# Window scores sorted by tile size, and the output projection behind the heads' transposes

## The chip, the cores and the metric

The kernel runs on one core of a Trainium2 chip. The metric is the device time of one execution in microseconds; lower is better. The engines are TensorE (PE for its matmuls, PEld for its weight loads, which overlap them), VectorE (DVE), ScalarE (ACT), GpSimd (POOL) and SyncE (SP), which issues the DMAs. Each engine works through its own instructions in order and waits on semaphores for the others.

## The reference

Thirty-two sequences of 128 tokens with 128 channels pass through one causal attention and one cross attention of 16 heads, and then through six layers of local attention and a gated MLP. The change lies in the local attention. Cut to what matters:

```python
for i in range(6):
    qkv = shift_tokens(x) @ Wqkv[i]                 # 128 -> 3 * 16 heads * 64
    q, k = rotary(l2norm(q) * q_scale), inverse_rotary(l2norm(k) * k_scale)
    # windows of 32 queries, each against its own 32 keys and the 32 before
    sim = einsum('bhwie,bhwje->bhwij', bq, bk2) * 8.0
    sim = where(mask, -max, sim)
    out = einsum('bhwij,bhwje->bhwie', softmax(sim, -1), bv2)
    x = out @ Wo[i] + x
    x = ffn_layer(shift_tokens(x)) + x
```

## The kernel before, in words

Each layer's local attention works through 128 groups: 32 sequences by four groups of four heads (64 channels each). One group enters in every step. A body of the loop holds `STEPS` = 8 steps, two sequences. The work of a group is spread over nine steps by hand-written lags (`WIN`), so one step of an engine holds pieces of several groups. TensorE's step, in the order of `win_products`:

- `win_project` (L735): queries and keys of group j, three matmuls of 512 columns, after it waits for the squares of the last group (`c_sq`).
- `win_turn_probs` (L791): two transposes of the probabilities of group j-7.
- `win_values` (L735): values of group j, three matmuls of 256 columns (`c_vproj`).
- `win_project_out` (L843): output projection of group j-8 from `prob_t`, four matmul records. It waits for ACT's copy of the head sums (`c_sum`) and, at a sequence's first group, for DVE's addition of the previous sequence's result into y (`c_yadd`).
- `win_heads` (L728): four transposes of the rotated queries and keys of group j-4. Ahead of the fourth, `sums_ready` makes PE wait for what the head sums below need: `c_vout` (ACT's copy of this step's values and turned probabilities), `c_scaled`, and for every second group `c_moved`.
- `win_mask` (L765): four bf16 matmuls with 64x64 tiles that put the band mask into PSUM.
- `win_scores` (L776): scores of group j-5, twelve matmuls in 24 records. A record is one pass of a matmul through the array; an f32 matmul of this kind has two. For each of two head pairs i, first two matmuls of 64x64 tiles (queries 0 to 63), then four of 64x32 tiles (queries 64 to 95, and 96 to 127). The last one signals `c_scores`.
- `win_sum_values` (L823): the head sums of group j-7, twelve matmuls with 64x64 tiles, 24 records.

A tile is the part of TensorE's array that one matmul uses, rows x columns. Matmuls with different tiles of one size run side by side.

ACT's step is `vout_all` (L1115, the copy of values and turned probabilities), `qk_t` (L1086, the copy of the turned heads), `squares` (L1095, after DVE's `by_sin`), four exponentials (L1104, after DVE's `top`) and `prob_t` (L1124, the copy of the head sums). DVE's step is `rsum` (L1595, after the exponentials), `prob` (L1605), `by_cos` (L1546), `by_sin` (L1554), `rotated` (L1563), `top` (L1587, the maxima, after `c_scores`), `norm` (L1570, after `squares`) and `norm2g` (L1580). In the fourth step of a sequence ACT also copies the next tokens (`xt_high`, L1075) behind `prob_t`, and DVE then makes `xt_low` (L1528) and adds to y (L1612) ahead of the next `rsum`. Of each layer's 128 steps, 123 run in `windowed`; the first five lie in the end of the layer before, beside its MLP. Eight more, without new projections, drain the pipeline (`drain`), and there the heads stand ahead of the output projection already.

Of the kernel before, what the change touches and what calls it, by code (L numbers as in the profile page):

```python
# [28 lines left out]
DH = 64  # L29
# [3 lines left out]
PAD = 32  # L33
# [39 lines left out]
KEYS = 2 * PAD  # L73
BASES = (0, PAD, 2 * PAD)
# [3 lines left out]
ENDED = GROUPS // STEPS  # L78
# [62 lines left out]
def has(index):  # L141

    return not isinstance(index, int) or index >= 0


def in_range(it, j, lag, n):

    return not isinstance(it, int) or 0 <= it * n[1] + j - lag < n[0]


def build(nc, x_in, ctx_in, a_w, a_m, b_wq, b_bq, b_wk, b_bk, b_wv, b_bv, b_wo, b_bo, wqkv, q_scale, k_scale,
          wo, ln_g, ln_b, w1, b1, w2, b2, const_d, out):
    with ExitStack() as stack:
        def sb(name, shape, dt=F32):
            return stack.enter_context(nc.sbuf_tensor(name, shape, dt))
# [11 lines left out]
        ident_b = sb("ident_b", [P, P], BF16)  # L167
        causal_b = sb("causal_b", [P, P], BF16)
        band_b = sb("band_b", [P, 2, KEYS], BF16)
# [88 lines left out]
        win_ps, sum_ps = [[t[:, :].rearrange("q (e n) -> q e n", e=2)[:, :, at:at + P] for t in (pair45, pair12)] for at in (0, P)]  # L258
# [16 lines left out]
        def sem(name):  # L275
            return stack.enter_context(nc.semaphore(name))
# [103 lines left out]
        c_scores = sem("c_scores")  # L380
# [70 lines left out]
        def here(it, j, lag):  # L451
            return in_range(it, j, lag, (GROUPS, STEPS))
# [125 lines left out]
        def _(pe):  # L578
# [138 lines left out]
            def win_heads(layer, it, j):  # L717
                if here(it, j, WIN.turn):
                    g = layer * GROUPS + it * STEPS + j - WIN.turn
                    jl = (j - WIN.turn) % STEPS  # L720
                    pe.wait_ge(c_unit, g + 1)
                    if has(it * STEPS + j - WIN.turn - 1):
                        pe.wait_ge(c_qk, g)
                    flat = rotated[jl % 4][:, :, :, :].rearrange("t a h d -> t (a h d)")
                    for k in range(4):
                        if k == 3 and not isinstance(it, int):
                            sums_ready(layer, it, j)
                        last = nc.tensor.transpose(heads_ps[:, k * P:(k + 1) * P], flat[:, k * P:(k + 1) * P], ident)  # L728
                    last.then_inc(c_heads, 1)

# [21 lines left out]
            def win_values(layer, it, j):  # L752
                if here(it, j, 0):
                    if has(it * STEPS + j - 1):

                        pe.wait_ge(c_vout, layer * VOUTS + it * STEPS + j)
                    gc = (j % NG) * HG * DH
                    split_product(value_ps[:, 2 * P:4 * P], j // NG, 2, slice(gc, gc + HG * DH)).then_inc(c_vproj, 1)

            def win_mask(layer, it, j):  # L760
                if here(it, j, WIN.scores):
                    for half in range(2):
                        for e in range(2):
                            rows, lower = slice(e * DH, (e + 1) * DH), half * DH
                            nc.tensor.matmul(win_ps[(j - WIN.scores) % 2][lower:lower + DH, e, :].rearrange("q (i k) -> q i k", i=2),  # L765
                                             ident_b[rows, rows], band_b[rows, half, :].unsqueeze(1).to_broadcast([DH, 2, KEYS]),
                                             start=True, stop=False, skip_group_check=True, tile_position=(e * DH, lower))

            def win_scores(layer, it, j):
                if here(it, j, WIN.scores):  # L770
                    jl = (j - WIN.scores) % STEPS
                    for i in range(2):
                        for lower, n, base in ((0, DH, BASES[0]), (DH, PAD, BASES[1]), (DH + PAD, PAD, BASES[2])):
                            for e in range(2):
                                rows, q0, k0 = slice(e * DH, (e + 1) * DH), i * P + lower, (2 + i) * P + base
                                last = nc.tensor.matmul(win_ps[jl % 2][lower:lower + n, e, i * KEYS:(i + 1) * KEYS],  # L776
                                                        qk_t[jl % 4][rows, q0:q0 + n], qk_t[jl % 4][rows, k0:k0 + KEYS],
                                                        start=False, stop=False, skip_group_check=True, tile_position=(e * DH, lower))
                    last.then_inc(c_scores, 1)

            def win_turn_probs(layer, it, j):
                if here(it, j, WIN.probs):
# [19 lines left out]
            def sums_ready(layer, it, j):  # L802

                if here(it, j, WIN.value):
                    jl = (j - WIN.value) % STEPS
                    if jl % 2 == 0:

                        pe.wait_ge(c_moved[jl // 2], 64 * (layer * ENDED + it + (1 if j >= WIN.value else 0)))
                    if here(it, j, WIN.scale):

                        pe.wait_ge(c_scaled, layer * GROUPS + it * STEPS + j - WIN.scale + 1)
                    pe.wait_ge(c_vout, layer * VOUTS + it * STEPS + j + 1)
# [15 lines left out]
            def win_project_out(layer, it, j):  # L828
                if isinstance(it, int) and it == 0 and j == STEPS - 1:
                    pe.wait_ge(s_wo_in, 16 * (layer + 1))  # L830
                if here(it, j, WIN.out):
                    m = layer * GROUPS + it * STEPS + j - WIN.out
                    jl = (j - WIN.out) % STEPS
                    b = it * 2 + (j - WIN.out) // NG
                    if jl % NG == 0:

                        if has(b - 1):
                            pe.wait_ge(c_yadd, layer * NB + b)
                        pe.wait_ge(c_xsplit, layer * NB + xt_before(b))
                    pe.wait_ge(c_sum, m + 1)  # L840
                    for i in range(2):
                        k = 2 * (jl % NG) + i
                        last = nc.tensor.matmul(acc_ps[:, 0:P], prob_t[(j - 1) % 2][:, i, :], wo_sb[:, k * P:(k + 1) * P],  # L843
                                                start=(k == 0), stop=(k == 2 * NG - 1))
                    if jl % NG == NG - 1:
                        last.then_inc(c_wo, 1)

            def xt_before(b):

                return min(NB, b + 4) if isinstance(b, int) else b + 4  # L850

            def win_products(layer, it, j):
                win_project(layer, it, j)
                win_turn_probs(layer, it, j)
                win_values(layer, it, j)
                win_project_out(layer, it, j)
                win_heads(layer, it, j)
                win_mask(layer, it, j)
                win_scores(layer, it, j)
                win_sum_values(layer, it, j)  # L860

            def win_step(layer, it, j):
                win_products(layer, it, j)
                win_turn_next(layer, it, j)
# [70 lines left out]
            def drain(layer):  # L935
                for j in range(WIN_DRAIN):
                    win_turn_probs(layer, ENDED, j)
                    win_heads(layer, ENDED, j)
                    win_project_out(layer, ENDED, j)
                    win_mask(layer, ENDED, j)  # L940
                    win_scores(layer, ENDED, j)
                    if j == 3:
                        mlp_turn(layer, 0, 1)
                    if j == 4:
                        mlp_turn(layer, 1, 0)
                    if j == 6:
                        mlp_up(layer, 1, 0)
                    win_sum_values(layer, ENDED, j)
                    if j == 6:
                        mlp_turn(layer, 1, 1)  # L950
                        mlp_up(layer, 1, 1)
                mlp_down(layer, 1, 1)
# [435 lines left out]
        def _(dve):  # L1388
# [193 lines left out]
            def win_max(layer, it, j):  # L1582
                if here(it, j, WIN.top):
                    m = layer * GROUPS + it * STEPS + j - WIN.top
                    slot = (j - WIN.top) % 2
                    dve.wait_ge(c_scores, m + 1)
                    nc.vector.tensor_reduce(top[slot][:, :].rearrange("q (e i) -> q e i", e=2), win_ps[slot].rearrange("q e (i k) -> q e i k", i=2),  # L1587
                                            AX_X, ALU.max, negate=True).then_inc(c_top, 1)

# [202 lines left out]
            with dve.Fori(0, NQ // 2) as q2:  # L1792
                for j in range(2):
                    q = q2 * 2 + j
# [9 lines left out]
                for j in range(2):  # L1804
                    q = q2 * 2 + j
# [45 lines left out]
```

## Time and profile before

| | |
|---|---|
| median of 3 runs | 4686.99 us (4685.81 to 4687.43) |
| profiled execution, its own time | 4686.16 us |
| its span | 4684.4 us |
| PE busy | 4212.9 us, 90% |
| PEld busy | 3257.4 us, 70% |
| DVE busy | 3681.5 us, 79% |
| ACT busy | 3240.9 us, 69% |
| POOL busy | 3109.8 us, 66% |

The span runs from the first instruction to the last; what lies around it is 1.8 us. Busy shares add up overlapping pieces, and matmuls are pipelined, so that the page's 90% for PE doesn't say that PE sets the pace. For that, the chain of waits is read in one step of the loop: which engine starts each piece as soon as something else has ended.

### The profile page before, as it was taken

What the parts mean: (1) busy time and instruction counts of PE and PEld (TensorE: products, weight loads), DVE (VectorE), ACT (ScalarE), POOL (GpSimd) and SP (SyncE); (2) the same over time, 40 slices, a digit from 0 to 9 for tenths busy, and PEclk for the clock granted to TensorE, in tenths of its full rate; (3) what the DMA queues carried; (4) which work ended last, traced back from release to release, by engine and by line L of the source; (5) the groups of instructions that cost most, each with busy time, mean ns of one, the idle gap of its engine ahead of it and who ended that gap; (6) DMA issues with size and microseconds to landing.
All of it is one profiled execution on the core that took longest, in us unless ns stands there. A gap on an engine that the chain in (4) does not pass through costs nothing.

```text
span 4684.4 us, 162974 instructions
## 1 busy us (share of the span) xinstructions
PE 4212.9 (90%) x60256; PEld 3257.4 (70%) x60256; DVE 3681.5 (79%) x9664; ACT 3240.9 (69%) x11601; POOL 3109.8 (66%) x2461
## 2 busy tenths in 40 slices
PE   7988868999889999899999899998899998999998
PEld 5666646777677777677777677776777776777776
DVE  7988877777777777687777687777777776877776
ACT  6889966777657777657777567776577775677774
POOL 4544457777657777667777577776677776677773
PEclk9999989999999999999999999999999999999999
DMA  2000001111111111111111111111111111111111
GB/s 75 0 0 1 0 14 33 29 29 28 33 48 30 29 29 29 32 49 29 28 28 29 35 47 29 29 29 32 49 30 29 28 29 33 35 29 29 29 30 41
DMA packets 301674, 140.09 MB, mean 30 GB/s; under 512 B 83988, under 2 KB 293778, under 8 KB 301458
## 3 DMA queue, kind: packets, MB, share of 16 engines
q1 hardware_dynamic: 301458, 137.25, 12.0%
q8 instruction: 130, 2.13, 0.2%
q14 instruction: 86, 0.70, 0.1%
HBM read 21.85 MB, written 2.10 MB: 5 GB/s over the span
## 4 chain that ended last, share of the span: by engine, by line
PE 40%; ACT 28%; DVE 22%; issue 8%; DVEq 1%; POOL 1%; SPq 0%; DMA 0%; ACTq 0%; POOLq 0%
ACT pair L1104 19%; PE pair L776 13%; PE bank L843 11%; DVE top L1587 7%; PE bank L728 6%; ACT prob_t L1124 6%; PE pair L899 3%; PE pair L765 3%; DVE top L1502 2%; DVE qk_parts L1477 2%; DVE by_cos L1546 1%; DVE by_sin L1554 1%; PE bank L915 1%; DVE by_sin L1470 1%; ACT prob L1029 1%
## 5 line engine op out<-in xcount | busy, mean ns | idle before, releaser
L1272 POOL TENSOR_TENSOR rnorm<-norm2g,neg_half 128x16 f32<-128x16 f32 x384 | 1115.4, 2905 | 366.7 <-DVE norm2g L1580 366.7
L1104 ACT ACTIVATE pair<-pair,top 128x64 f32<-128x64 f32 x3072 | 879.1, 286 | 390.1 <-DVE top L1587 390.1
L1264 POOL TENSOR_TENSOR rotated<-by_cos,by_sin 128x256 f32<-128x256 f32 x768 | 696.7, 907 | 567.4 <-DVE by_sin L1554 563.4
L1086 ACT ACTIVATE qk_t<-bank 128x512 f32<-128x512 f32 x768 | 459.2, 598 | 606.9 <-PE bank L728 606.6
L776 PE MATMUL pair<-qk_t 64*32 64x64 f32 (+1 forms) x18432 | 798.5, 230 | 0.0
L1285 POOL TENSOR_TENSOR rotated<-rotated,rnorm 128x512 f32<-128x512 f32 x768 | 784.6, 1042 | 0.5
L843 PE MATMUL bank<-wo_sb,prob_t 128*128 128x128 f32 x3072 | 548.8, 302 | 240.7 <-ACT prob_t L1124 131.2
L843 PEld LDWEIGHTS bank<-wo_sb,prob_t 128*128 128x128 f32 x3072 | 403.8, 191 | 398.2 <-ACT prob_t L1124 304.7
L735 PE MATMUL bank<-wqkv_high,xt_high 128*128 128x512 f32 (+1 forms) x1536 | 663.1, 432 | 17.2 <-ACT squares L1095 16.1
L776 PEld LDWEIGHTS pair<-qk_t 64*32 64x32 f32 (+1 forms) x18432 | 538.6, 114 | 175.5 <-issue 1.4
L1104 ACT ACTIVATION_READ_ACCUMULATOR pair<-pair,top 128x1 f32 x3072 | 625.7, 204 | 0.0
L1546 DVE TENSOR_TENSOR by_cos<-bank,rot_cos 128x512 f32<-128x512 f32 x768 | 522.7, 681 | 6.2 <-PE bank L735 6.1
L735 PE MATMUL bank<-wqkv_low,xt_high 128*128 128x512 f32 (+1 forms) x1536 | 524.7, 342 | 0.0
L1570 DVE TENSOR_REDUCE norm<-squares 128x8 f32<-128x512 f32 x768 | 520.2, 677 | 3.5 <-ACT squares L1095 3.5
L1554 DVE TENSOR_TENSOR by_sin<-bank,sin_now 128x512 f32<-128x512 f32 x768 | 522.8, 681 | 0.0
L735 PE MATMUL bank<-wqkv_high,xt_low 128*128 128x512 f32 (+1 forms) x1536 | 521.7, 340 | 0.0
L1115 ACT ACTIVATE vout_all<-bank 128x512 f32<-128x512 f32 (+1 forms) x810 | 468.0, 578 | 76.1 <-PE bank L735 58.3
L1095 ACT ACTIVATE squares<-bank 128x512 f32<-128x512 f32 x768 | 456.0, 594 | 42.6 <-DVE by_sin L1554 39.5
L1254 POOL TENSOR_TENSOR kz_parts<-qk_parts,cst 128x512 fp32r<-128x512 f32 x256 | 266.2, 1040 | 308.4 <-DVE qk_parts L1477 308.4
L728 PE MATMUL bank<-cst,rotated 128*128 128x128 f32 x3072 | 469.0, 276 | 0.0
L1587 DVE TENSOR_REDUCE top<-pair 128x4 f32<-128x256 f32 x768 | 325.7, 424 | 177.8 <-PE pair L776 159.7
L823 PE MATMUL pair<-vout_all 64*64 64x64 f32 x6096 | 423.0, 232 | 33.7 <-issue 33.7
(152 smaller groups left out, 9044.2 us busy)
## 6 DMA issues: line engine op xcount, KB each, us to landing
vmoved<-vout_all SPq DMA_DIRECT2D x1152, 64.0 KB, 2.1
ctx_all<-vout_all SPq DMA_DIRECT2D x384, 64.0 KB, 2.1
wqkv_sb<-in_L_ffn_Wqkv_dram SPq DMA_DIRECT2D x36, 256.0 KB, 3.8
ctx_all<-y SPq DMA_DIRECT2D x48, 128.0 KB
ctx_all<-y SPq DMA_DIRECT2D x48, 127.0 KB
wo_sb<-in_L_ffn_Wo_dram SPq DMA_DIRECT2D x6, 512.0 KB, 10.2
out_dram<-y SPq DMA_DIRECT2D x8, 256.0 KB, 3.5
w_sb<-in_L_ffn_W_dram SPq DMA_DIRECT2D x6, 341.0 KB, 3.2
```

What stands on the lines that cost most here:

```text
L728: last = nc.tensor.transpose(heads_ps[:, k * P:(k + 1) * P], flat[:, k * P:(k + 1) * P], ident)
L735: last = nc.tensor.matmul(dst, a[slot][:, :], w[:, which, cols], start=(n == 0), stop=(n == 2))
L776: last = nc.tensor.matmul(win_ps[jl % 2][lower:lower + n, e, i * KEYS:(i + 1) * KEYS], qk_t[jl % 4][rows, q0:q0 + n], qk_t[jl % 4][rows, k ...
L843: last = nc.tensor.matmul(acc_ps[:, 0:P], prob_t[(j - 1) % 2][:, i, :], wo_sb[:, k * P:(k + 1) * P], start=(k == 0), stop=(k == 2 * NG - 1))
L1104: last = nc.scalar.activation(at, at, ACT.Exp, bias=top[jl % 2][:, h:h + 1], accum_out=psum_raw[jl % 2][:, h:h + 1])
L1264: nc.gpsimd.tensor_tensor(rotated[j % 4][:, 1, :, :], by_cos[j % 2][:, 1, :, :], by_sin[j % 2][:, 1, :, :], ALU.add).then_inc(c_rot, 1)
L1272: nc.gpsimd.tensor_tensor(rnorm[slot][:, :, :].rearrange("t g n -> t (g n)"), norm2g[slot][:, :, :].rearrange("t g n -> t (g n)"), neg_hal ...
L1285: nc.gpsimd.tensor_tensor(at, at, rnorm[slot][:, i, :].unsqueeze(2).to_broadcast([P, 2 * HG, DH]), ALU.mult).then_inc(c_unit, 1)
L1546: nc.vector.tensor_tensor(by_cos[j % 2][:, :, :, :], got, table(rot_cos, layer).unsqueeze(2).to_broadcast([P, 2, HG, DH]), ALU.mult).then_ ...
L1554: nc.vector.tensor_tensor(rows(by_sin[j % 2]), got, rows(sin_now), ALU.mult).then_inc(c_sin, 1)
L1570: nc.vector.tensor_reduce(pair[:, :, 0:1], squares[:, :, :], AX_X, ALU.add).then_inc(c_nrm2, 1)
L1587: nc.vector.tensor_reduce(top[slot][:, :].rearrange("q (e i) -> q e i", e=2), win_ps[slot].rearrange("q e (i k) -> q e i k", i=2), AX_X, A ...
```

## The change

The masks and scores of a group are now sorted by tile size. `win_upper_scores` does queries 64 to 127 with 64x32 tiles: four masks, then eight matmuls. `win_lower_scores` does queries 0 to 63 with 64x64 tiles: two masks, then four matmuls. The head sums, 64x64 too, follow. The masks are six matmuls instead of four, since the upper half's two are cut into four. Each of the two calls signals `c_scores`, and DVE waits for both. In a step of `windowed`, the heads' transposes come ahead of the output projection, and the waits of `sums_ready` move from the heads' fourth transpose to between the two matmuls of the output projection. In the drain only the sorting applies.

```diff
@@ win_heads
                     for k in range(4):
-                        if k == 3 and not isinstance(it, int):
-                            sums_ready(layer, it, j)
@@ scores
-            def win_scores(layer, it, j):
+            def win_scores(layer, it, j, tiles):
                 if here(it, j, WIN.scores):
                     jl = (j - WIN.scores) % STEPS
+                    for lower, n, base in tiles:
+                        for e in range(2):
+                            rows, upper = slice(e * DH, (e + 1) * DH), lower // DH
+                            at = e * DH + lower % DH
+                            nc.tensor.matmul(win_ps[jl % 2][lower:lower + n, e, :].rearrange("q (i k) -> q i k", i=2),
+                                             ident_b[rows, at:at + n], band_b[rows, upper, :].unsqueeze(1).to_broadcast([DH, 2, KEYS]),
+                                             start=True, stop=False, skip_group_check=True, tile_position=(e * DH, lower))
                     for i in range(2):
-                        for lower, n, base in ((0, DH, BASES[0]), (DH, PAD, BASES[1]), (DH + PAD, PAD, BASES[2])):
+                        for lower, n, base in tiles:
...
+            def win_upper_scores(layer, it, j):
+                win_scores(layer, it, j, ((DH, PAD, BASES[1]), (DH + PAD, PAD, BASES[2])))
+
+            def win_lower_scores(layer, it, j):
+                win_scores(layer, it, j, ((0, DH, BASES[0]),))
@@ win_project_out
                     for i in range(2):
                         k = 2 * (jl % NG) + i
+                        if i and not isinstance(it, int):
+                            sums_ready(layer, it, j)
@@ win_products
+                win_heads(layer, it, j)
                 win_project_out(layer, it, j)
-                win_heads(layer, it, j)
-                win_mask(layer, it, j)
-                win_scores(layer, it, j)
+                win_upper_scores(layer, it, j)
+                win_lower_scores(layer, it, j)
                 win_sum_values(layer, it, j)
@@ VectorE, win_max
-                    dve.wait_ge(c_scores, m + 1)
+                    dve.wait_ge(c_scores, 2 * m + 2)
```

TensorE's queue in a step of the loop, before, from the output projection to the scores. In these rows `bank` and `pair` are PSUM, the sizes are contraction or output rows by columns, and the semaphores waited for stand in brackets:

```order
L843 MATMUL bank<-wo_sb,prob_t 128x128 [waits c_sum_copied]
L843 MATMUL bank<-wo_sb,prob_t 128x128
L728 MATMUL bank<-cst,rotated 128x128 [waits c_qk_ready,c_unit]
L728 MATMUL bank<-cst,rotated 128x128 x2
L812 REGISTER_ALU [waits c_scaled,c_values_moved3]
L728 MATMUL bank<-cst,rotated 128x128 [waits c_vout_ready]
L765 MATMUL pair<-band_b,ident_b 64x128 x4
L776 MATMUL pair<-qk_t 64x64 x2
L776 MATMUL pair<-qk_t 32x64 x4
L776 MATMUL pair<-qk_t 64x64 x2
L776 MATMUL pair<-qk_t 32x64 x4
```

And the same place now:

```order
L726 MATMUL bank<-cst,rotated 128x128 [waits c_qk_ready,c_unit]
L726 MATMUL bank<-cst,rotated 128x128 x3
L847 MATMUL bank<-wo_sb,prob_t 128x128 [waits c_sum_copied]
L814 REGISTER_ALU [waits c_scaled,c_values_moved3]
L847 MATMUL bank<-wo_sb,prob_t 128x128 [waits c_vout_ready]
L765 MATMUL pair<-band_b,ident_b 32x128 x4
L772 MATMUL pair<-qk_t 32x64 x8
L765 MATMUL pair<-band_b,ident_b 64x128 x2
L772 MATMUL pair<-qk_t 64x64 x4
```

The transposes have moved ahead of the wait for `c_sum`, the wait for `c_vout` has moved from the last transpose into the output projection, and the tile size changes once inside the scores instead of three times.

In the drain, TensorE's queue of a step before, from the heads to the first head sums:

```order
L728 MATMUL bank<-cst,rotated 128x128 [waits c_qk_ready,c_unit]
L728 MATMUL bank<-cst,rotated 128x128 x3
L843 MATMUL bank<-wo_sb,prob_t 128x128 [waits c_sum_copied]
L843 MATMUL bank<-wo_sb,prob_t 128x128
L765 MATMUL pair<-band_b,ident_b 64x128 x4
L776 MATMUL pair<-qk_t 64x64 x2
L776 MATMUL pair<-qk_t 32x64 x4
L776 MATMUL pair<-qk_t 64x64 x2
L776 MATMUL pair<-qk_t 32x64 x4
```

There the order of heads and output projection stays, and only the mask and score rows are sorted, as above.

## Rows read from the trace of the kernel before

**Rows 1.** Chain of waits: start us, us, engine and line; one loop step.

```profile
2498.72 0.71 PE bank L843 x4
2499.43 0.44 PE bank L728 x4
...
2500.98 0.44 DVE top L1587
2501.44 1.15 ACT pair L1104 x7
2502.61 0.40 ACT prob_t L1124
```

**Rows 2.** Timeline of PE: start us, us, line, output<-inputs, tile, idle before and releaser.

```profile
2503.06 0.71 PE L843 MATMUL bank<-wo_sb,prob_t 128*128 128x128 f32 x4 [0.19 <-ACT prob_t L1124]
```

**Rows 3.** Timeline of DVE over one body of eight steps, maxima and rotated queries.

```profile
2486.98 0.42 DVE L1587 TENSOR_REDUCE top<-pair 128x4 f32<-128x256 f32 x1 [0.26 <-PE pair L776]
...
2492.31 0.42 DVE L1587 TENSOR_REDUCE top<-pair 128x4 f32<-128x256 f32 x1
...
2496.14 0.42 DVE L1563 TENSOR_TENSOR rotated<-by_cos,by_sin 128x256 f32<-128x256 f32 x1
2496.65 0.42 DVE L1587 TENSOR_REDUCE top<-pair 128x4 f32<-128x256 f32 x1
...
2502.76 0.18 DVE L1595 RECIPROCAL rsum<-psum_raw 128x4 f32<-128x4 f32 x1 [0.47 <-ACT pair L1104]
...
2504.63 0.43 DVE L1563 TENSOR_TENSOR rotated<-by_cos,by_sin 128x256 f32<-128x256 f32 x1
2505.32 0.42 DVE L1587 TENSOR_REDUCE top<-pair 128x4 f32<-128x256 f32 x1 [0.26 <-PE pair L776]
...
2509.83 0.42 DVE L1563 TENSOR_TENSOR rotated<-by_cos,by_sin 128x256 f32<-128x256 f32 x1
2510.37 0.42 DVE L1587 TENSOR_REDUCE top<-pair 128x4 f32<-128x256 f32 x1
...
2523.38 0.42 DVE L1587 TENSOR_REDUCE top<-pair 128x4 f32<-128x256 f32 x1 [0.26 <-PE pair L776]
```

**Rows 4.** Timeline of DVE at the first layer's start, ahead of the first output projection.

```profile
722.44 0.42 DVE L1587 TENSOR_REDUCE top<-pair 128x4 f32<-128x256 f32 x1
...
726.09 0.42 DVE L1563 TENSOR_TENSOR rotated<-by_cos,by_sin 128x256 f32<-128x256 f32 x1
726.43 0.42 DVE L1587 TENSOR_REDUCE top<-pair 128x4 f32<-128x256 f32 x1
```

**Rows 5.** The same stretch on PE and on ACT.

```profile
722.75 0.50 PE L735 MATMUL bank<-wqkv_high,xt_high 128*128 128x512 f32 x1 [1.63 <-ACT squares L1095]
...
724.39 0.60 ACT L1115 ACTIVATE vout_all<-bank 128x512 f32<-128x512 f32 x1 [0.20 <-PE bank L735]
```

**Rows 6.** Timeline of PE in narrow windows: masks, scores and head sums by tile.

```profile
2504.14 0.25 PE L765 MATMUL pair<-band_b,ident_b 64*64 64x128 bf16 x4
2504.22 0.28 PE L776 MATMUL pair<-qk_t 64*64 64x64 f32 x4
...
2504.43 0.32 PE L776 MATMUL pair<-qk_t 64*32 64x64 f32 x8
...
2504.67 0.33 PE L776 MATMUL pair<-qk_t 64*64 64x64 f32 x4
...
2505.18 0.27 PE L823 MATMUL pair<-vout_all 64*64 64x64 f32 x1
...
2505.51 0.22 PE L823 MATMUL pair<-vout_all 64*64 64x32 f32 x1
```

**Rows 7.** Timeline of ACT, the copy of the values in that step.

```profile
2502.91 0.60 ACT L1115 ACTIVATE vout_all<-bank 128x512 f32<-128x512 f32 x1
```

**Rows 8.** Waits in all, longest first: us in total, times, longest us.

```profile
PEld bank L843 <- ACT prob_t L1124: 304.7, 641, 1.2
...
DVE top L1587 <- PE pair L776: 159.7, 493, 2.6
```

More of the change, by code:

```diff
@@ L758, in win_values @@
                     split_product(value_ps[:, 2 * P:4 * P], j // NG, 2, slice(gc, gc + HG * DH)).then_inc(c_vproj, 1)
[L760 to L767, printed above, removed]
-            def win_scores(layer, it, j):
+            def win_scores(layer, it, j, tiles):
                 if here(it, j, WIN.scores):
                     jl = (j - WIN.scores) % STEPS
+                    for lower, n, base in tiles:
[5 more added lines that the diff above has]
+                                             start=True, stop=False, skip_group_check=True, tile_position=(e * DH, lower))
                     for i in range(2):
-                        for lower, n, base in ((0, DH, BASES[0]), (DH, PAD, BASES[1]), (DH + PAD, PAD, BASES[2])):
+                        for lower, n, base in tiles:
                             for e in range(2):
@@ L939, in drain @@
                     win_project_out(layer, ENDED, j)
-                    win_mask(layer, ENDED, j)
-                    win_scores(layer, ENDED, j)
+                    win_upper_scores(layer, ENDED, j)
+                    win_lower_scores(layer, ENDED, j)
                     if j == 3:
```

## The prediction, on record before the changed kernel ran

> **What bounds the kernel now.** I first read the chain of waits in one step of the loop [rows 1]. It goes round in a circle: output projection 0.71 us, heads' transposes 0.44, masks and scores from 2499.87 to 2500.98, the maxima on DVE 0.44, the exponentials on ACT 1.15, the copy `prob_t` 0.40. Then the next output projection starts at 2503.06 [rows 2], 4.34 us after the last one. So PE's 90% busy is not the bound: PE stands still for 0.19 us ahead of the output projection, released by ACT's `prob_t` [rows 2], and the wait shows in nearly every step as the hold of the weight load, 641 times [rows 8]. The transposes stand in the circle only because they are queued behind the output projection.
>
> Second, DVE over one body of eight steps [rows 3]. From the maxima at 2486.98 to those at 2523.38 it takes 36.40 us. In most steps DVE is idle 0.26 us until PE's scores are done; the view of waits has that 493 times, 159.7 us [rows 8]. The body's steps, from maxima to maxima, are 5.33 us (a sequence's end, where y is added, and the loop's branch), 4.34, 4.33, 4.34, 5.05 (the other sequence's end) and three of about 4.34. The 5.33 step already ends with the maxima right behind other DVE work, without idle time. It gains nothing.
>
> **What would be next.** DVE and ACT have a circle of their own: maxima, exponentials, `rsum`, `prob`, `by_cos`, `by_sin`, `rotated`, maxima. The trace shows it unhindered at a layer's start, before any output projection is there: maxima at 722.44, `rotated` at 726.09, maxima 0.34 behind it at 726.43 [rows 4]. That is 3.99 us. In the steady loop the same pieces read: maxima 2500.98 [rows 1] to `rotated` 2504.63 is 3.65, plus 0.34 is again 3.99, where the maxima actually start at 2505.32, 4.34 after [rows 3]. No order on PE can go below that. In one step the circle is longer: from 2492.31 to `rotated` 2496.14 plus 0.34 is 4.17 instead of 4.34 [rows 3]. At the sequence's end in mid-body it is from 2505.32 to 2509.83 plus 0.34, that is 4.85 instead of 5.05 [rows 3].
>
> **The change part by part.** *Heads ahead of the output projection.* The transposes leave the circle through `prob_t`: 4.34 less 0.44 is 3.90 for it. While PE transposes, `prob_t` is being copied, so the 0.19 of standing still is covered too. `c_unit`, which the transposes wait for, comes from GpSimd in the group's third or fourth step, and they read it in the fifth; the buffer they write was emptied one step before. I cost that at nothing.
>
> *The moved wait.* `sums_ready` now stands ahead of the second half of the output projection. Behind it on PE are the masks, the scores and the head sums, and DVE's maxima wait for the scores. The last to come is `c_vout`. Before, the copy `vout_all` ran from 2502.91 to 2503.51 [rows 7], 0.75 after `rsum` started at 2502.76 [rows 3], and the wait stood late enough to be free. Now it decides. The state to come is shown at the layer's start, where the values' projection is held by `squares` (1.63 idle) and the copy starts at 724.39 [rows 5], 1.95 after the maxima of 722.44 [rows 4]. So, counted from the maxima: copy 1.95 to 2.55, PE released at about 2.60. From there to the masks: before, four records of output projection and four transposes took from 2503.06 [rows 2] to 2504.14 [rows 6], 1.08; less six records of 0.11 (0.44 by four [rows 1]) that leaves 0.42 with the tile switch. Masks at 3.02.
>
> *Sorting.* In the old order the sets start at 2504.22 (64x64), 2504.43 (64x32), 2504.67 (64x64), and the head sums at 2505.18 after one more 64x32 set; masks at 2504.14 [rows 6]. From 2504.43 to 2504.67 is 0.24 for two passes and a change of size. The head sums, all of one size, put six passes of four records between 2505.18 and 2505.51 [rows 6], about 0.06 a pass. So a change of size costs about 0.12 more than going on. New: masks 0.08, four upper passes with one change 0.24 + 2 x 0.06 = 0.36, lower masks 0.08 (taken like the first ones), four lower passes 0.24: 0.76 us to the head sums instead of 1.04. The last score pass starts 0.70 after the masks. Before it started 0.89 after them (2505.18 less the 0.15 of the last change and start). That is 0.19 sooner. The maxima started 1.18 after the masks (2505.32 less 2504.14); now they could 0.99 after. The two masks more are in this. Bounds for the section, as seen by the maxima: 0.19 gained if the passes keep the 0.06, nothing gained if the changes removed had only hidden something else; I take 0.19, since the 0.06 is measured on tiles used again and again, as here.
>
> Sum for a plain step: 3.02 + 0.99 = 4.01 by way of the moved wait, 3.99 by way of DVE, 3.90 - 0.19 = 3.71 by way of `prob_t`. The step is 4.01, and PE's own work, 4.34 - 0.19 - 0.28 = 3.87, fits in.
>
> Here a figure of the Trainium skill speaks against the change. The head sums' 24 records between 2505.18 and 2505.51 are 14 ns apart on average [rows 6]. The Trainium skill (TensorE: Matmul & The Clock Gate, "Wait — 56ns, not 53.3ns?") gives about 62 ns of sequencer time for each matmul when hardware decode is off; the trace disagrees. By that price the two masks more would put 0.12 into the path, the step would be 4.13, and the time would come to some 4550. By these rows I give that price a chance of 0.01, inside the case between forecast and first rival.
>
> **The sum.** Per body: 5.33 stays; 4.34 to 4.17 saves 0.17; five plain steps save 0.33 each, 1.65; the sequence's end 5.05 to 4.85 saves 0.20, since PE is held there by y and has its scores ready before DVE wants them. Together 2.02 us of 36.40. There are 123 steps per layer in `windowed`, 6 layers, 738 steps, 92 bodies: 186 us. The first steps of a layer already run at 3.99 and the code ahead of the loop has the same steps, so this may be a few us too much. In the drain only the sorting acts, 0.19 in three or so steps whose chain goes through the scores, times 6: 3 us. The two attentions ahead and the MLP are untouched. 4686.16 - 186 - 3 = 4497. The profiled execution is 0.8 below the median of the runs, which I neglect.
>
> **The rivals.**
>
> *The wait keeps the bound, the sorting gives nothing.* The plain step is then 4.01 + 0.19 = 4.20. Six steps save 0.14 each, the sequence's end 0.20: 1.04 by 92 is 96 us, 4590. For it: the path through `vout_all` and the one through DVE differ by 0.02 us only, so every hundredth that the path is underestimated shows. Against: the 0.06 per pass.
>
> *Slower.* The passes on the same tiles don't follow at 0.06. Upper passes now run four in a row on the same four tiles, and lower ones four in a row on only two, with weights changed each time. Six such intervals stand ahead of the last pass. The step is back at 4.34 when they cost 0.33 more, that is at 0.115 each instead of 0.06. At 0.16 the step is 4.01 + 6 x 0.10 = 4.61, 0.27 longer in six steps of eight, and the time is about 4686 + 149 = 4835. The head sums at 0.06, with the same four tiles reused, speak against it; for two tiles of 64 columns the trace has only pairs of passes.
>
> *No change.* Another chain holds 4.34, and heads and sorting are both hidden by it. It would need a wait that is now within 0.01 of the circle without being in it. The 3.99 at a layer's start speaks against it, though there the output projection is missing. 4678 to 4695.
>
> *More than forecast.* The steps in which DVE's circle takes 4.17 or longer may do so only because of how PE's work falls. If they too went to 3.99, and the 5.33 by as much, another 0.36 x 92 = 33 us: 4464.
>
> That the change does not do what it says is ruled out by the order of PE's instructions, which shows both moves in the loop's body.
>
> **Chances.** Forecast, 4475 to 4530: 0.64. Wait or passes between, 4530 to 4600: 0.21. More than forecast: 0.05. No change: 0.04. Slower: 0.06. The range for 8 in 10 reaches from 4464, the further case of DVE, to 4590, where sorting gives nothing. Under 0.2%, 9 us, a measurement of this kernel can't tell from no change; faster by more than that has 0.90, within it 0.04, slower 0.06.
>
> **What would show it.** The maxima should follow `rotated` by 0.34 in plain steps, with no idle time left to PE in most of them, and stand 3.99 to 4.03 apart. The idle time in front of the output projection's first record should be gone, and a new one should stand inside it, ended by ACT's `vout_all`. ACT's wait for the heads should nearly vanish and its wait for `by_sin` ahead of `squares` grow; PE's projection should start to wait for `squares`. From the first mask to the first head sum it should be 0.76 us. If that stretch is 0.9 or more, the sorting step is wrong; if it is right and the maxima still wait for PE, the moved wait is.

## The result

| | before | changed |
|---|---|---|
| median | 4686.62 us (4 runs, 4685.81 to 4687.43) | 4498.4 us (4 runs, 4497.05 to 4500.48) |
| ratio | | 0.9599, 95% interval 0.9582 to 0.9615 |
| span of the profiled execution | 4684.4 us | 4498.7 us |
| granted clock, mean | 0.984 | 0.980 |

The change makes the kernel 188 us faster. The forecast was 4497, in a range of 4464 to 4590. The clock doesn't explain the gain: the granted clock is a little lower now, 0.980 instead of 0.984. With its two levels, 2.4 and 1.2 GHz, that is 180 instead of 150 us at the lower one, so by this estimate it costs at most some 15 us.

The timeline of DVE in the changed kernel shows one plain step, from maxima to maxima. It answers to [rows 3] and [rows 4]:

```profile
2403.98 0.42 DVE L1591 TENSOR_REDUCE top<-pair 128x4 f32<-128x256 f32 x1
...
2405.76 0.18 DVE L1599 RECIPROCAL rsum<-psum_raw 128x4 f32<-128x4 f32 x1 [0.22 <-ACT pair L1108]
...
2407.63 0.42 DVE L1567 TENSOR_TENSOR rotated<-by_cos,by_sin 128x256 f32<-128x256 f32 x1
2407.97 0.42 DVE L1591 TENSOR_REDUCE top<-pair 128x4 f32<-128x256 f32 x1
```

The maxima start 0.34 us behind `rotated` and 3.99 after the last ones, and no idle time stands in front of them. That is DVE's own circle. PE in the same step, in the timeline (the last two rows overlap):

```profile
2406.06 0.98 PE L847 MATMUL bank<-wo_sb,prob_t 128*128 128x128 f32 x4
2406.96 0.24 PE L765 MATMUL pair<-band_b,ident_b 64*32 64x128 bf16 x4
2407.03 0.39 PE L772 MATMUL pair<-qk_t 64*32 64x64 f32 x16
2407.35 0.24 PE L765 MATMUL pair<-band_b,ident_b 64*64 64x128 bf16 x2
2407.43 0.34 PE L772 MATMUL pair<-qk_t 64*64 64x64 f32 x6
2407.56 0.27 PE L825 MATMUL pair<-vout_all 64*64 64x64 f32 x1
...
2407.61 0.22 PE L772 MATMUL pair<-qk_t 64*64 64x64 f32 x2
```

The last pass of the scores starts 0.65 us after the masks and ends at 2407.83. In a run further down DVE does wait for the scores in nearly every step (maxima first), and there it starts 0.92 after the first mask. So the maxima could have started at 2407.88; they did at 2407.97. PE is ahead of DVE, but by 0.09 us only.

The waits in all (us, times, longest): those that the forecast named, ACT's for the values' projection, and the one that was to go:

```profile
ACT squares L1099 <- DVE by_sin L1558: 640.6, 757, 1.9
...
PEld bank L733 <- ACT squares L1099: 146.9, 447, 2.0
PEld bank L847 <- ACT vout_all L1119: 123.0, 464, 0.4
...
ACT vout_all L1119 <- PE bank L733: 61.5, 41, 2.9
...
DVE top L1591 <- PE pair L772: 31.2, 27, 2.3
```

The view counts 27 waits of DVE for the scores instead of 493 [rows 8]. ACT's wait for `by_sin` was 39.5 us before. PE waits now for `squares`, ahead of the projection, and for `vout_all`, inside the output projection.

ACT's wait for the turned heads, 606.6 us before, has all but gone. The page's group of that copy, to its right the idle time before it:

```profile
L1090 ACT ACTIVATE qk_t<-bank 128x512 f32<-128x512 f32 x768 | 469.8, 612 | 5.4 <-PE bank L726 5.1
```

### The profile page after: what moved, and what is told of

It reads as the page before. It is cut to its first block, busy times and chain, and to the rows that moved or that the text cites. A ratio compares the mean times of both kernels' runs of the same rounds, so it can differ in the third digit from the quotient of the medians.

```text
span 4498.7 us, 166670 instructions
## 1 busy us (share of the span) xinstructions
PE 4006.1 (89%) x61792; PEld 3187.6 (71%) x61792; DVE 3629.1 (81%) x9664; ACT 3219.3 (72%) x11601; POOL 3113.0 (69%) x2461
## 4 chain that ended last, share of the span: by engine, by line
PE 44%; DVE 28%; ACT 16%; issue 10%; DVEq 1%; POOL 1%; SPq 0%; ACTq 0%; DMA 0%; POOLq 0%
PE bank L733 16%; DVE by_cos L1550 7%; DVE by_sin L1558 6%; PE bank L847 6%; PE bank L726 6%; ACT pair L1108 6%; ACT squares L1099 5%; PE pair L903 4%; PE pair L772 3%; PE bank L793 3%; PE pair L765 3%; DVE top L1506 3%; DVE top L1591 2%; DVE qk_parts L1481 2%; PE pair L825 2%
## 5 line engine op out<-in xcount | busy, mean ns | idle before, releaser
L847 PE MATMUL bank<-wo_sb,prob_t 128*128 128x128 f32 x3072 | 691.6, 315 | 163.8 <-DVE y L1616 56.1
L847 PEld LDWEIGHTS bank<-wo_sb,prob_t 128*128 128x128 f32 x3072 | 451.2, 190 | 355.3 <-ACT vout_all L1119 123.0
L772 PE MATMUL pair<-qk_t 64*32 64x64 f32 (+1 forms) x18432 | 610.6, 218 | 0.0
L825 PE MATMUL pair<-vout_all 64*64 64x64 f32 x6096 | 453.3, 226 | 37.8 <-issue 37.8
L1090 ACT ACTIVATE qk_t<-bank 128x512 f32<-128x512 f32 x768 | 469.8, 612 | 5.4 <-PE bank L726 5.1
L772 PEld LDWEIGHTS pair<-qk_t 64*32 64x32 f32 (+1 forms) x18432 | 459.9, 116 | 0.0
L733 PEld LDWEIGHTS bank<-wqkv_high,xt_high 128*128 128x128 f32 x1536 | 290.5, 189 | 207.6 <-ACT squares L1099 146.9
```

The source lines that it names most:

```text
L733: last = nc.tensor.matmul(dst, a[slot][:, :], w[:, which, cols], start=(n == 0), stop=(n == 2))
L825: last = nc.tensor.matmul(out_ps[e * DH:(e + 1) * DH, lower:lower + width], values_of(j, i, e, n), vout[j][rows, e * P + lower:e * P + low ...
```

## The experiments

Each run is set beside the kernel before, timed next to it on the same chip. A step is the median time from maxima to maxima of the plain steps of a body; where two values stand, they alternate. Gains over the kernel before are taken against the time in the same row. The chips differ by up to 6 us for the same kernel, so between rows of different chips the ratios are the safer measure.

| kernel | median us | before, beside it | ratio, 95% interval | plain step us |
|---|---|---|---|---|
| changed | 4498.4 | 4686.6 | 0.9599 (0.9582 to 0.9615) | 3.99 |
| sorting only | 4534.5 | 4689.4 | 0.9670 (0.9654 to 0.9686) | 4.07 |
| move only | 4612.5 | 4689.4 | 0.9834 (0.9818 to 0.9850) | 4.18 and 4.26 |
| wait left in the heads | 4666.5 | 4689.4 | 0.9950 (0.9933 to 0.9967) | 4.19 and 4.28 |
| changed, maxima first | 4439.3 | 4689.4 | 0.9462 (0.9446 to 0.9478) | 3.90 and 3.99 |
| the same, third wait apart | 4436.1 | 4683.6 | 0.9473 (0.9457 to 0.9488) | 3.90 and 3.98 |
| before, maxima first | 4700.5 | 4683.6 | 1.0036 (1.0022 to 1.0050) | 4.34 |
| changed, by_cos first | 4618.1 | 4683.6 | 0.9858 (0.9841 to 0.9874) | 4.07 and 4.17 |
| changed, both edits | 4875.9 | 4683.6 | 1.0411 (1.0394 to 1.0429) | 4.50 and 4.67 |
| sorting only, two changes | 4614.4 | 4684.4 | 0.9851 (0.9834 to 0.9867) | 4.23 |
| sorting only, lower first | 4545.9 | 4684.4 | 0.9706 (0.9690 to 0.9723) | 4.10 |

### Sorting alone, moving alone

Sorting only, against the changed kernel:

```diff
                     for k in range(4):
+                        if k == 3 and not isinstance(it, int):
+                            sums_ready(layer, it, j)
...
-                        if i and not isinstance(it, int):
-                            sums_ready(layer, it, j)
...
-                win_heads(layer, it, j)
                 win_project_out(layer, it, j)
+                win_heads(layer, it, j)
```

> The changed kernel with the order of before for heads and output projection and with the wait for the values' copy in the heads' fourth transpose; only the sorting by tile size stays. If PE's circle through prob_t (4.34 us a step) sets the pace here, the sorting shortens it by what the scores finish sooner: 0.19 as forecast, 0.24 if the last score pass starts 0.65 us after the masks as the changed kernel's trace shows. Steps of 4.15 or 4.10, five or six of eight, and the time 4560 to 4570 or 4535 to 4545. If the gain came from the move alone and the sorting only followed, the step stays at 4.34 and the time at 4687.

4534.5 us: 155 us of gain, most of what both edits bring. The chain of waits shows PE's circle again, as in [rows 1], with the scores shortened:

```profile
2250.22 0.71 PE bank L847 x4
2250.93 0.44 PE bank L728 x4
2251.37 0.17 PE pair L767 x4
2251.53 0.22 PE pair L774 x16
2251.76 0.17 PE pair L767 x2
2251.93 0.18 PE pair L774 x6
2252.21 0.44 DVE top L1591
2252.67 1.12 ACT pair L1108 x7
2253.85 0.40 ACT prob_t L1128
2254.29 0.71 PE bank L847 x4
```

From output projection to output projection it is 4.07, and 0.27 of the 4.34 has gone. The masks and scores take 0.84 (2251.37 to 2252.21) where they took 1.11. The expectation's second figure, 4.10, was near; its first, from the forecast's 0.19, was too small.

Move only, against the kernel before:

```diff
-                        if k == 3 and not isinstance(it, int):
-                            sums_ready(layer, it, j)
...
+                        if i and not isinstance(it, int):
+                            sums_ready(layer, it, j)
...
+                win_heads(layer, it, j)
                 win_project_out(layer, it, j)
-                win_heads(layer, it, j)
```

> The kernel of before with heads ahead of the output projection and the wait moved into it; masks and scores unsorted. The path through the moved wait was put at 4.01 with the sorting; without it 4.20, and the time 4590. The changed kernel's trace has the scores ready 0.07 us before DVE takes them (a path of 3.92), and unsorted scores end 0.24 later: 4.16, and the time 4570 to 4580. If DVE's own circle of 3.99 were all that counts once the heads are out of the way, the time would be 4500 as with the sorting.

4612.5 us, 77 us of gain. The plain steps take 4.18 and 4.26 in turn; the forecast's 4.20 for this very case is met in the step. In time it came out 22 us slower than 4590, since the sequences' ends (5.01 and 5.39 against 4.86 and 5.33 in the changed kernel) and the step behind the longer one (4.34 against 4.17) are longer too. A step without idle time in front of the maxima would be 3.99, so here PE's path is the bound, and the expectation's third case, 4500, falls.

Together the two make 155 + 77 = 232 us, but both at once gained 188. The missing 44 us are put down to DVE's circle, which is tested below. Only some 11 of them are missing in the bodies: there sorting alone saves 1.69 us, moving alone 0.51 and both 2.08, by the medians of the eight steps. Much of the rest is missing in a layer's first and last steps, which take 3.99 by the move alone already and 3.99 in the changed kernel too.

### Where the wait stands

The wait left in the heads, against the changed kernel:

```diff
                     for k in range(4):
+                        if k == 3 and not isinstance(it, int):
+                            sums_ready(layer, it, j)
...
-                        if i and not isinstance(it, int):
-                            sums_ready(layer, it, j)
```

> The changed kernel with the wait for the values' copy left in the heads' fourth transpose, as before, heads ahead of the output projection. If that wait is as close to the bound as the trace says (path 3.92 by it), one transpose and four records instead of two then stand behind it, 0.44 us more: a step of 4.36, and the time 4670 to 4700, the whole gain gone. If the wait is not near the bound, the time stays at 4498.

4666.5 us: only 23 us of the gain are left, by a wait that stands three matmul records earlier in PE's queue. The waits in all show the new first line on PE, and beside it a second one that was not expected, for DVE's `prob`:

```profile
PEld bank L728 <- ACT vout_all L1119: 494.5, 563, 1.5
...
PE bank L728 <- DVE prob L1609: 210.1, 198, 1.6
```

A transpose and the whole output projection now stand behind the wait. The plain step is 4.19 and 4.28, less than the 4.36 expected. The expectation had an error: three records of 0.11 us more behind the wait are 0.33, not 0.44, and 3.92 + 0.33 = 4.25 is what was measured. The sequences' ends, 5.17 and 5.66 against 4.86 and 5.33, add to it. A whole body takes 36.4 us, as in the kernel before; the 23 us come from a layer's first and last steps, which run at 3.99. So inside the loop the place of this wait is worth as much as the whole change.

### The floor under DVE's circle

DVE's step, against the changed kernel:

```diff
-                win_rotate_queries(layer, it, j)
                 win_max(layer, it, j)
+                win_rotate_queries(layer, it, j)
                 win_norms(layer, it, j)
```

> The changed kernel with DVE's maxima ahead of the rotated queries, which takes 0.34 us out of DVE's circle (3.99 to 3.65) and leaves all work in. If DVE's circle sets the changed kernel's pace, the next bound is PE's path through the values' copy at 3.92: 0.07 less in six steps of eight, up to 0.17 more in the first two steps of a body, 40 to 70 us in all, 4430 to 4460. If PE's path is the bound already (4.01 as forecast), the time stays within 10 us of 4498.

4439.3 us, 59 less than the changed kernel, by an edit that only swaps two instructions on DVE. DVE's timeline now has the maxima waiting for PE:

```profile
2209.42 0.42 DVE L1591 TENSOR_REDUCE top<-pair 128x4 f32<-128x256 f32 x1 [0.37 <-PE pair L772]
...
2213.37 0.42 DVE L1591 TENSOR_REDUCE top<-pair 128x4 f32<-128x256 f32 x1 [0.26 <-PE pair L772]
...
2217.36 0.42 DVE L1591 TENSOR_REDUCE top<-pair 128x4 f32<-128x256 f32 x1 [0.38 <-PE pair L772]
```

So DVE's circle did set the changed kernel's pace, and the path through the moved wait lies at 3.90 and 3.99 in turn (here 3.95 and 3.99), not at 4.01. With the floor lowered, the sum also closes roughly: 250 us of gain against 232 for the two edits apart, of which some 27 come from steps that DVE bound before as well (5.33 to 5.13 and 4.17 to 4.08, times 92 bodies). This version beats both kernels.

The same swap in the kernel before:

> The kernel of before with the same edit on DVE, maxima ahead of the rotated queries. In the kernel before, PE's circle through prob_t is the bound (4.34) and DVE's circle of 3.99 has 0.35 to spare; only the first step of a body and the one at its end are bound by DVE. So 0.17 at the most in one or two steps of eight, 0 to 30 us: 4660 to 4690. If DVE's order mattered in itself, as it did for the changed kernel (59 us), the gain would be the same 59 us, 4630.

4700.5 us, 17 slower. Where DVE's circle is not the bound, the swap brings nothing, as expected; the 5.33 step, which DVE does bound, falls to 5.23. That the swap costs something on the whole was not expected. One step of eight takes 4.62 instead of 4.34, and the rotated queries now stand behind a wait of DVE for PE:

```profile
2318.20 0.42 DVE L1587 TENSOR_REDUCE top<-pair 128x4 f32<-128x256 f32 x1 [0.63 <-PE pair L776]
2318.54 0.41 DVE L1563 TENSOR_TENSOR rotated<-by_cos,by_sin 128x256 f32<-128x256 f32 x1
```

By which way the later queries reach that one step was not followed up.

The alternation of 3.90 and 3.99 might come from the third wait of every second group. That wait apart, against the changed kernel with the maxima first:

```diff
-                    if jl % 2 == 0:
+                    if jl % 2 == 0 and isinstance(it, int):
...
+                        if k == 2 and not isinstance(it, int) and here(it, j, WIN.value) and (j - WIN.value) % 2 == 0:
+                            pe.wait_ge(c_moved[(j - WIN.value) % STEPS // 2], 64 * (layer * ENDED + it + (1 if j >= WIN.value else 0)))
...
```

> The changed kernel with the maxima first, and with the wait for the moved values (every second group) taken out of the output projection and put ahead of the heads' third transpose; the waits for prob and for the values' copy stay. With the maxima first, the plain steps take 3.90 and 3.99 in turn. If the third wait behind the output projection's first half costs the 0.09, all plain steps come to 3.90 and the time falls by 4 x 0.09 x 92, 33 us at the most, 4405 to 4425. If the alternation is DVE's, nothing changes, 4439.

4436.1 us, and 3.90 and 3.98 in turn. The ratios, 0.9473 and 0.9462, lie in each other's intervals: no difference. That wait is not the cause. The timeline of the run with the maxima first shows that the 0.09 arises ahead of it: the copy `vout_all` starts 2.00 us after the maxima in the steps of 3.99 (2213.37 to 2215.36) and 1.90 after them in those of 3.90 (2226.10 to 2228.00). What delays the copy in every second step stays open.

### DVE's idle time filled, and what that shows

DVE's step, against the changed kernel:

```diff
+                win_cos(layer, it, j)
                 win_recip(layer, it, j)
                 win_scale(layer, it, j)
-                win_cos(layer, it, j)
                 win_sin(layer, it, j)
```

> The changed kernel with DVE's by_cos ahead of rsum and prob, where DVE stands idle for the exponentials (0.47 a step). That takes as much as 0.47 out of DVE's circle by another edit. If the floor under DVE's circle is PE's path through the values' copy (3.90 and 3.99 in turn, as with the maxima first), the time comes to the same 4430 to 4450. If the maxima's early start did something else in that run, the two differ: 4498 still, or well under 4430.

4618.1 us, 120 slower than the changed kernel. The expectation was wrong. The moved wait is not for the values' copy alone. `sums_ready` waits for `prob` of this step as well, and with `by_cos` (0.68 us) in front of it, where the changed kernel has 0.41 us of idle time on average (233.4 us in 564 waits), `prob` ends later. The plain steps take 4.07 and 4.17 instead of 3.99, and the sequences' ends 5.34 and 5.83 instead of 4.86 and 5.33: the ends make up 0.99 of some 1.6 us that a body gets longer. The timeline of PE at a sequence's end, the second half of the output projection:

```profile
2201.71 0.48 PE L847 MATMUL bank<-wo_sb,prob_t 128*128 128x128 f32 x2 [0.41 <-DVE y L1616]
2203.25 0.48 PE L847 MATMUL bank<-wo_sb,prob_t 128*128 128x128 f32 x2 [1.06 <-DVE prob L1609]
2203.66 0.28 PE L765 MATMUL pair<-band_b,ident_b 64*32 64x128 bf16 x4
2203.73 0.64 PE L772 MATMUL pair<-qk_t 64*32 64x64 f32 x16
```

In the whole run PE's records have 195.1 us of idle time ended by `prob` on this line, in 367 waits. The changed kernel has 30.8 us in 92 waits. On top of it TensorE's clock falls. The same sixteen records took 0.39 in the changed kernel and 0.64 here. The stretches around it, with the busy time of each engine and the granted clock after POOL's:

```profile
2200.00:2203.20 3.20, 1.78 (x13) 1.26 (x11) 1.79 (x6) 1.98 (x8) 2.90 (x1) 1.00 0.13 31
2203.20:2207.20 4.00, 3.95 (x61) 3.21 (x62) 2.13 (x5) 2.17 (x10) 2.98 (x3) 0.57 0.00 0
2207.20:2212.00 4.80, 4.47 (x79) 3.85 (x78) 4.00 (x10) 3.09 (x12) 1.54 (x2) 1.00 0.22 51
```

The clock is the smaller part. In the whole run it is 0.974 against 0.980, some 60 us more at the lower level, which by this estimate cost 30 of the 120 us at the most.

Both edits together:

> Both edits on DVE in the changed kernel. If PE's path is the floor, the second edit brings nothing: 4425 to 4445. If DVE's circle were still the bound with one edit, it falls by another 0.3 us a step, 4250 to 4350.

4875.9 us, slower than the kernel before, and far from both figures expected. With both edits DVE waits for PE's scores before it rotates the queries, and PE waits for DVE's `prob` before it makes the scores of the next step:

```profile
DVE top L1591 <- PE pair L772: 628.8, 715, 2.3
...
PE bank L847 <- DVE prob L1609: 488.6, 599, 1.5
```

So DVE's circle is not a sum of pieces from which any may be taken: what stands in the place of the piece decides who waits next.

### What a change of tile size costs

Against sorting only, the upper scores of the second head pair (`pairs`) moved behind the lower ones. The diff leaves out how `win_scores` uses its three new arguments:

```diff
...
             def win_upper_scores(layer, it, j):
-                win_scores(layer, it, j, ((DH, PAD, BASES[1]), (DH + PAD, PAD, BASES[2])))
+                win_scores(layer, it, j, ((DH, PAD, BASES[1]), (DH + PAD, PAD, BASES[2])), pairs=(0,))
...
-                win_scores(layer, it, j, ((0, DH, BASES[0]),))
+                win_scores(layer, it, j, ((0, DH, BASES[0]),), signal=False)
+                win_scores(layer, it, j, ((DH, PAD, BASES[1]), (DH + PAD, PAD, BASES[2])), masks=False, pairs=(1,))
```

> The sorting-only kernel (order and wait of before) with one change of tile size more inside the scores: upper masks and upper scores of the first pair, lower masks and all lower scores, upper scores of the second pair, then the head sums. Same matmuls. Steps took 4.34 with three changes inside the scores and 4.07 with one. If each change ahead of the last score pass costs the same, half the gain goes, a step of 4.20 and a time of 4605 to 4615. If the sorting's gain comes from something else (the masks, two tiles instead of six at a time), the time stays near 4534 or jumps back to 4687.

4614.4 us and a step of 4.23. Three changes of size inside the scores make 4.34, two 4.23, one 4.07, with the same scores and, between the last two, the same masks too. PE's timeline in this kernel:

```profile
2286.89 0.24 PE L767 MATMUL pair<-band_b,ident_b 64*32 64x128 bf16 x4
2286.96 0.28 PE L774 MATMUL pair<-qk_t 64*32 64x64 f32 x8
2287.17 0.24 PE L767 MATMUL pair<-band_b,ident_b 64*64 64x128 bf16 x2
2287.25 0.64 PE L774 MATMUL pair<-qk_t 64*64 64x64 f32 x16
```

One more change costs 0.16. Of that 0.14 is the later start of the last score pass, 0.79 instead of 0.65 after the masks; the rest lies between that pass and the maxima. From three changes to two only 0.11 is gained; there the kernel with three has two masks fewer, which may be the difference of 0.05, but no run takes the masks apart.

Lower tiles first, against sorting only:

```diff
+                win_lower_scores(layer, it, j)
                 win_upper_scores(layer, it, j)
-                win_lower_scores(layer, it, j)
...
```

The same swap is made in the drain.

> The sorting-only kernel with the lower 64x64 tiles first and the upper 64x32 tiles behind them, so that the size changes once inside the scores, as there, and once more between scores and head sums. If PE's circle ends at the scores, a change behind them is hidden in PE's slack, and the time is that of sorting only, 4525 to 4545. If PE's whole work counts, 0.15 to 0.3 a step come back, 4580 to 4640.

4545.9 us, a step of 4.10. A change of size now stands between scores and head sums as well, and it is hidden there. The ratio is 0.0036 above that of sorting only, 17 us, just clear of both intervals: 0.03 a step. The change behind the scores isn't the cause of these 0.03, for the last score pass starts 0.65 after the masks in both kernels. They lie between that pass and the maxima, which start 0.29 after it here, where it is one of 64x32 tiles, and 0.27 after it in the kernel with sorting only, where it is one of 64x64. So PE's work after the scores is off the path, and the work up to them is on it.

## Why the prediction was right, point by point

**The bound before.** The circle through the output projection, the transposes, the scores, the maxima, the exponentials and `prob_t` [rows 1] was the bound. Sorting alone shortens it by the 0.27 by which the scores finish sooner. Moving alone takes the transposes out of it, and the path through the moved wait takes over at 4.18 and 4.26.

**The next bound.** The circle of DVE and ACT at 3.99, read from a layer's start [rows 4] and from the pieces of a steady step [rows 3], is exactly what the changed kernel runs at. Body by body its steps are 3.99 five times, 4.17, 4.86 and 5.33, where the forecast had 4.01, 4.17, 4.85 and 5.33. The swap of two DVE instructions, which shortens that circle and leaves PE's queue as it is, confirms that it was the bound, by 59 us.

**The moved wait.** The forecast had the path through `vout_all` at 4.01 and took it for the bound by 0.02. That was wrong, if by little: the path is 3.90 and 3.99, and DVE's circle is the bound. Of the difference 0.05 is the copy, which starts 1.90 after the maxima (2403.98 to 2405.88) and not 1.95, and 0.07 is the sorting, below. The step from the released wait to the masks was 0.42 in the sum, and it is 0.41: in the changed kernel the second half starts at 2402.56 and the masks at 2402.97. That the wait is that near to the bound is shown by the run in which it stays in the heads, and by the one in which `prob` comes later. What the forecast didn't see is how near the second of its semaphores, `c_scaled`, is to the first. It said that the last to come is `c_vout`; in the changed kernel it is `prob` in 92 steps, most of them at the longer of a body's two sequence ends.

**Sorting.** This is the term that was too small. The last pass of the scores was to start 0.70 after the masks and starts 0.65 after them; the head sums were to start at 0.76 and start at 0.60, because they begin while the lower scores still run. By the program the lower scores leave two of the four tiles free; the trace doesn't say which tile a record uses. The scores' end comes 0.27 sooner by the step, where 0.19 was forecast. The changed kernel can't use the difference, since DVE's circle is the floor, and so the sum came out right: 2.08 us a body (36.39 to 34.31) where 2.02 was forecast, and 188 us where 189 was. That it came out to 1 us is in part luck. Two terms were off, the copy and the sorting, both hidden by a floor that lay 0.02 below the forecast's step, and the bodies alone make 191 us, so that the rest of the kernel gained nothing where 3 were forecast.

**The rivals.** "The wait keeps the bound, the sorting gives nothing" had 4.20 for the move without the sorting; measured 4.18 and 4.26. Its premise fell. "Slower", by passes that don't follow each other at 0.06 on the same tiles: sixteen upper records start within 0.18 us (0.39 for all of them, of which one takes 0.22), four passes less than 0.06 apart. On the lower scores' two tiles, of which the forecast had only pairs of passes, the four passes start from 2407.43 to 2407.61, 0.06 apart. "No change" and "more than forecast" needed a chain at 4.34 and a DVE circle that gives way; the steps of 3.99, 4.17 and 5.33 show neither. The figure of the Trainium skill (TensorE: Matmul & The Clock Gate, "Wait — 56ns, not 53.3ns?"), about 62 ns a matmul with hardware decode off, would by estimate spread the starts of these eight upper matmuls over 0.43 us, or over 0.93 if each of the sixteen records counts as one. The trace has 0.18, so this price isn't paid here; no run shows whether hardware decode was on.

## What to carry to other kernels

Find the circle of waits that gives the period, and then the next one, from a stretch where the first is absent: it says how much an edit can bring before it is made. An edit on the first circle is worth no more than the distance to the second, so that two good edits may add to less than their sum, and the swap of two instructions on another engine then brings the rest. In a queue that runs in order, the place of a wait can be worth as much as the order of the work, and each of the semaphores in it has to be checked.

## What the runs showed of the hardware

- One more change of tile size inside the scores made the step 0.16 us longer (4.07 to 4.23). Across the change the starts lie 0.15 us apart (2287.43 to 2287.58 in the run with two changes), against 0.06 between passes of one size. Behind the scores, where PE's work is off the path, a change was hidden.
- Matmuls that come later in PE's queue can start before the last passes of those ahead, where the size is the same: the first head sums at 2407.56, the last lower scores at 2407.61.
- The maxima start 0.27 us after the start of the last score pass when that is one of 64x64 tiles, 0.28 to 0.29 after it when it is one of 64x32 (medians over some 500 steps of a run).
- The clock's level of 1.2 GHz came after a stretch in which PE was busy 1.78 of 3.20 us. Over the next 4.00 us the mean granted clock was 0.57, and sixteen records took 0.64 instead of 0.39. So that wait on PE cost more than its length.
